# Three moves in an interleaved attention pipeline: a merge and its sum one step later in odd slots, and two SBUF elementwise operations from VectorE to GpSimd

## The chip, the cores and the metric

The kernel runs on 1 core of one Trainium2 chip. The metric is the device time of one execution in microseconds (us). Before the change the median of 3 runs is 2411.21 us (2408.04 to 2418.13).

## The reference, cut to what matters

The input x has 16 sequences of 512 tokens of 128 numbers, in fp32. Two blocks are added to it, each of a layernorm of what came before.

```python
x = x + _L0_attn_ref(_layernorm(x), wq, wk, wv, wo)   # causal, 16 heads of 8, rotary q and k
x = x + _L0_ffn_ref(_layernorm(x), wqkv, ...)          # 2 layers, each:
    h = shift_token(x);  q, k, v = split(h @ wqkv)     # 8 heads of 64
    q = l2norm(q) * qs;  k = l2norm(k) * ksc;  q, k = rotary_xpos(q, k)
    o = local_attention(q, k, v)                       # window 64 and the one before
    x = x + o @ wo
    h = layernorm(shift_token(x)) * lg + lb
    a, g = split(h @ w1 + b1);  x = x + (a * gelu(g)) @ w2 + b2
```

The outer `x +` of the second line is what the code calls adding X1 to the output: X1 is the result of the first line, Z the running value of the two layers.

## The kernel before, in words

The 16 sequences are worked on as 8 pairs (i = 0 to 7), and a pair has 16 slots (s = 0 to 15), one for each tile of 128 tokens: two layers, two sequences (z = 0, 1), four tiles. `bodies` writes the slots out in a row for every engine: two pairs of slots that only fill the pipeline (i = -2, -1), the eight real ones, and 4 slots that empty it. A program of an engine is therefore fixed by the order of calls in the loop `for s in slots` of its block, and engines meet only in semaphores. `past(sem, value)` is a wait that turns into a trivial one at the start.

In one slot s of pair i these run interleaved:
- the second block for tile s: scores (PE L725, L734), row maxima `nm` and subtraction `PX` (DVE L1019, L1022), exp (ACT L1223), transposes (PE L554), P times V (PE L751), division (DVE L1034, L1037), and for the tile before it, s-1, the turn of the heads (`turn_o`, copied by ACT L1233 to OT), `merge` (PE L786, o @ wo) and `add_heads` (DVE L1046, adds it to Z); for tile s+3 the projection (PE L699), copied by ACT L1214 to RAW, squares (ACT L1219) and `norms` (DVE L1029); for tile s+2 on Pool `over_norms` (a power, L1408) and the two rotary products and their sum (L1384, L1395, L1401), which give RC; `unit_heads` (DVE L1012) makes QN of RC one slot later.
- in odd slots the first part of the MLP of half a sequence (`half_turn`, `gates` L801, gelus on ACT L1260, `last_chunk` L810), in even slots its second part (`ups` L819, `down` L828, `add_mlp` L1082).
- `attention_step(s, pos)`, pos = 0 to 5: the first block's causal attention of later pairs, 16 heads by 2 sequences, cut into three chunks per head (512; 384 with 128; 256 columns), one chunk per step. PE makes scores for the maximum (L587) and, 6 heads later, scores for the exponential (L600, L602) in one PSUM bank each. DVE takes the maxima (L977, `maxed`), ACT the exponentials (L1188, `exped`). With one bank for each, L587 waits for the DVE of the step before, and L600 for the ACT of the step before.
- every second slot a unit of four heads goes through its maxima on Pool (`maxima_parts`, L1365 to L1371), the transpose on PE (`turn_maxima`, L622) and P times V (L645).
- the first block's projections two pairs ahead. Their rotary rows `rope_t` are split in three bf16 parts: `next_high` (ACT L1160) rounds, `next_rest` (DVE L953, slots 3, 5, 11 and 13) subtracts what was rounded, `next_middle` (ACT L1164) rounds the rest, and `next_low` (DVE L957) the last part. Then they go out through DRAM.
- layernorms of the first block on Pool: `next_normalise` in slots 1 and 9, `first_normalise` at the end of slot 7 and in slot 15 (L1338, L1340).

The last layer's `add_mlp` also adds X1 (kept in DRAM, brought back to XR) to the result: DVE L1087, in slots 12 and 14 and in slots 0 and 2 of the next pair. `fin` tells the SP queue that XR can be stored. All DMAs that these sentences speak of are issued by SP.

Of the kernel before, what the change touches and what calls it, by code (L numbers as in the profile page):

```python
# [135 lines left out]
def tile_in(i, m):  # L136

    return lives(i, m // ITEMS)
# [32 lines left out]
def build(nc, t, out):  # L171
    with ExitStack() as ctx:
# [374 lines left out]
        def _(pe):  # L547
# [28 lines left out]
            def body(i, slots):  # L576
# [260 lines left out]
                for s in slots:  # L837
# [15 lines left out]
                    if tile_in(i, s - 1):  # L853
                        merge(s - 1)
                    attention_step(s, 1)
                    attention_step(s, 2)
# [59 lines left out]
        def _(v):  # L916
# [34 lines left out]
            def next_rest(n, z, w):  # L951
                v.wait_ge(*past(part_hi.sem[z], part_hi.at(n, w + 1)))
                v.tensor_tensor(rope_s[:, :], rope_t[:, :], qkp[:, w, 0, :], ALU.subtract).then_inc(part_res.sem[z], 1)  # L953

# [15 lines left out]
            def body(i, slots):  # L970
# [70 lines left out]
                def add_heads(m):  # L1041
                    l, z, tt = place(m)
                    src = Z[z] if l else Z_first[z]
                    v.wait_ge(*past(x_tr.sem, x_tr.at(i, m // HT - 1)))
                    v.wait_ge(*past(wo_mm.sem, wo_mm.at(i, m + 1)))
                    v.tensor_tensor(Z[z][:, tt, :], m_ps[:, 0:D], src[:, tt, :], ALU.add).then_inc(z_acc.sem, 1)  # L1046
# [31 lines left out]
                def add_mlp(p):  # L1078
# [5 lines left out]
                    if l == L - 1:  # L1084
                        v.wait_ge(*past(x1_back[h].sem, x1_back[h].at(later(i, p // PIECES), z + 1)))
                        v.wait_ge(*past(z_out.sem, z_out.at(i, p + 1)))
                        v.tensor_tensor(XR[h][:, :, :], XR[h][:, :, :], zh, ALU.add).then_inc(fin.sem[h], 1)  # L1087

                for s in slots:
# [16 lines left out]
                    if tile_in(i, s - 1):  # L1106
                        add_heads(s - 1)
                    attention_step(s, 1)
                    attention_step(s, 2)
                    if s % 8 == 3 and lives(i, 2):  # L1110
                        next_rest(two, z, 0)
                    if s % 8 == 5 and lives(i, 2):
                        next_rest(two, z, 1)
# [210 lines left out]
        def _(g):  # L1324
# [24 lines left out]

            def first_normalise(k, z):  # L1350
# [6 lines left out]
            def body(i, slots):  # L1357
# [51 lines left out]

                def tile_normalise(m):  # L1410
# [11 lines left out]
                for s in slots:  # L1422
# [3 lines left out]
                    if s % 2 == 0 and unit_in(i, s // 2 + 10):  # L1426
                        maxima_parts(s // 2 + 10)
                    if s % 8 == 1 and lives(i, 2):
                        next_normalise(later(i, 2), s // 8)
# [86 lines left out]
```

## Time and profile before

| | before |
|---|---|
| median of 3 runs | 2411.21 us |
| lowest, highest | 2408.04, 2418.13 us |
| the profiled execution's own time | 2418.14 us |
| its span | 2416.4 us |
| TensorE clock granted in it | 0.977 of full speed |
| busy: PE, DVE, ACT, Pool | 2140.1, 1698.7, 1561.1, 1826.3 us |
| instructions | 55022 |

The span is that of the instructions of one execution, the time also holds what lies around it. No engine is busy all the time, so that the table alone names no limit; it has to be looked for in the waits and in the order of one slot.

### The profile page before, as it was taken

The numbers are of one execution on the slowest core, as the hardware profiler recorded it, in microseconds if no ns is written. First come the engines' busy times: TensorE is split into PE (matmuls) and PEld (weight loads), VectorE is DVE, ScalarE is ACT, GpSimd is POOL, SyncE is SP. The second block draws the span as 40 slices with busy tenths as digits, with TensorE's granted clock in tenths as the row PEclk, the third lists the DMA queues.
The fourth block names the chain that finished last, engine by engine and source line by source line (L and its number), as shares of the span: only waits on it lengthen the run. The fifth ranks groups of instructions, "written<-read, shape, count | busy, mean of one in ns | idle before, by whom it ended". The sixth has DMA issues, their size and how long they took to land.

```text
span 2416.4 us, 55022 instructions
## 1 busy us (share of the span) xinstructions
PE 2140.1 (89%) x20736; PEld 1463.9 (61%) x20736; DVE 1698.7 (70%) x4504; ACT 1561.1 (65%) x2510; POOL 1826.3 (76%) x1743
## 2 busy tenths in 40 slices
PE   4887889999999989999999989999899999988886
PEld 1444666666666666666666656666666666665664
DVE  4766777777777877777777777777777776655553
ACT  1545666676677667667676766766676677765553
POOL 2126879797887978788797978879687887798992
PEclk9998999999999999999999999999999999999997
DMA  4222111121212211121111212121111211111010
GB/s 139 67 63 57 43 51 50 45 60 45 58 37 61 52 45 51 47 61 44 51 50 48 57 44 58 35 63 52 40 51 47 61 46 38 25 33 28 21 32 23
DMA packets 115082, 119.56 MB, mean 49 GB/s; under 512 B 31946, under 2 KB 88055, under 8 KB 114819
## 3 DMA queue, kind: packets, MB, share of 16 engines
q1 hardware_dynamic: 114818, 116.04, 18.4%
q8 instruction: 167, 2.74, 0.5%
q14 instruction: 97, 0.79, 0.1%
HBM read 55.96 MB, written 20.97 MB: 32 GB/s over the span
## 4 chain that ended last, share of the span: by engine, by line
PE 50%; DVE 20%; POOL 14%; issue 10%; ACT 4%; DMA 1%; SPq 0%; DVEq 0%; POOLq 0%; ACTq 0%
DVE ps L977 6%; PE ps L554 6%; PE ps L645 5%; PE ps L734 4%; PE ps L751 4%; PE ps L587 4%; PE ps L712 4%; PE ps L828 3%; DVE nm L1019 3%; POOL inv L1408 3%; PE ps L699 3%; PE ps L600 3%; PE ps L567 2%; PE ps L819 2%; PE ps L810 2%
## 5 line engine op out<-in xcount | busy, mean ns | idle before, releaser
L977 DVE CUSTOM_DVE_ANT_0 ps<-ps,causal 128x512 f32<-128x512 f32 (+3 forms) x1024 | 491.2, 504 | 310.0 <-PE ps L587 307.1
L1188 ACT ACTIVATE PT<-ps 128x512 f32<-128x512 f32 (+1 forms) x768 | 406.8, 534 | 362.4 <-PE ps L602 350.1
L1408 POOL TENSOR_TENSOR inv<-ss,nhalf 128x16 f32<-128x16 f32 x128 | 378.7, 2959 | 324.6 <-DVE QN L1012 320.0
L587 PE MATMUL ps<-KA,QA 72*128 72x512 bf16 (+3 forms) x1024 | 274.7, 310 | 113.7 <-DVE nmax L977 111.8
L1395 POOL TENSOR_TENSOR RS<-RAW,rot 128x512 f32<-128x512 f32 x256 | 330.1, 1311 | 0.0
L1401 POOL TENSOR_TENSOR RC<-RC,RS 128x1024 f32<-128x1024 f32 x128 | 301.4, 2355 | 18.4
L1384 POOL TENSOR_TENSOR RC<-RAW,rot 128x1024 f32<-128x1024 f32 x128 | 302.7, 2365 | 0.0
L600 PE MATMUL ps<-QA,KA 75*128 75x512 bf16 (+3 forms) x1024 | 285.5, 304 | 10.6 <-ACT PT L1188 9.0
L699 PE MATMUL ps<-wqkv,ZT 128*128 128x512 f32 x512 | 241.1, 593 | 0.0
L1019 DVE TENSOR_REDUCE nm<-ps 128x8 f32<-128x1024 f32 x128 | 156.3, 1221 | 112.3 <-PE ps L734 112.2
L587 PEld LDWEIGHTS ps<-KA,QA 72*128 72x128 bf16 x1024 | 99.3, 100 | 208.8 <-DVE nmax L977 145.5
L1029 DVE TENSOR_REDUCE ss<-SQ 128x16 f32<-128x1024 f32 x128 | 155.5, 1215 | 89.1 <-POOL inv L1408 80.9
L1247 ACT COPY V_odd<-ps 128x512 f32<-128x512 f32 x128 | 74.9, 585 | 213.0 <-PE ps L712 210.2
L602 PE MATMUL ps<-causal_t,identb 128*128 128x128 bf16 x1024 | 200.7, 222 | 0.0
L786 PEld LDWEIGHTS ps<-wo,OT 128*128 128x128 f32 x1024 | 134.1, 191 | 63.0 <-issue 57.4
L1223 ACT ACTIVATE PX<-PX 128x1024 f32<-128x1024 f32 x128 | 136.5, 1067 | 55.2 <-DVE PX L1022 54.5
L645 PE MATMUL ps<-PT,V 128*32 128x512 f32 (+3 forms) x2048 | 161.3, 458 | 8.5 <-ACT PT L1188 2.3
L1022 DVE TENSOR_TENSOR PX<-ps,nm 128x1024 f32<-128x1024 f32 x128 | 156.7, 1224 | 4.4
L1012 DVE TENSOR_TENSOR QN<-RC,inv 128x1024 f32<-128x1024 f32 x128 | 157.5, 1231 | 0.2 <-POOL RC L1401 0.2
L600 PEld LDWEIGHTS ps<-QA,KA 75*128 75x128 bf16 x1024 | 101.2, 99 | 81.2 <-ACT PT L1188 27.4
L554 PE MATMUL ps<-ident,PX 128*128 128x128 f32 x1024 | 138.5, 280 | 12.1 <-ACT PX L1223 12.1
L751 PE MATMUL ps<-V_even,PT 128*64 128x65 f32 x2048 | 147.3, 225 | 0.4
(122 smaller groups left out, 5237.3 us busy)
## 6 DMA issues: line engine op xcount, KB each, us to landing
V_even<-V_odd SPq DMA_DIRECT2D x256, 130.0 KB, 2.4
QA<-parts SPq DMA_DIRECT2D x192, 96.0 KB
KA<-parts SPq DMA_DIRECT2D x192, 96.0 KB
parts<-qkp SPq DMA_DIRECT2D x32, 384.0 KB, 3.5
X_next<-in_x SPq DMA_DIRECT2D x16, 256.0 KB, 3.1
X<-in_x SPq DMA_DIRECT2D x16, 256.0 KB, 2.9
x_kept<-X SPq DMA_DIRECT2D x16, 256.0 KB, 3.6
XR<-x_kept SPq DMA_DIRECT2D x32, 128.0 KB, 2.7
```

What stands on the lines that cost most here:

```text
L554: last = pe.transpose(dst[:, tt * P:(tt + 1) * P], src(tt), ident[:, :])
L587: last = pe.matmul(dst[:, c0:c0 + w], QA[e][0:QK_ROWS, h % UNIT, qt * P:(qt + 1) * P], KA[e][0:QK_ROWS, h % UNIT, 0:w], start=True, stop=True)
L600: pe.matmul(dst[:, c0:c0 + w], KA[e][0:ROWS, h % UNIT, kt * P:(kt + 1) * P], QA[e][0:ROWS, h % UNIT, kt * P:S], start=True, stop=False)
L645: last = pe.matmul(a_ps[32 * n:32 * (n + 1), kt * P:S], V1[z][:, kt, h * VW:h * VW + 32], PT1[:, n, c0:c0 + w], start=(kt == 0), stop=(kt ...
L699: mm = pe.matmul(ps[:, w, :], ZT[z][:, tt * P:(tt + 1) * P], wqkv[:, l, w * INNER:(w + 1) * INNER], start=True, stop=True)
L751: mm = pe.matmul(out_ps[b * WIN:(b + 1) * WIN, h // PAIR2, h % PAIR2, :], PT[:, h % 2, h // 2, b * WIN:(b + 1) * WIN], values[:, h, :], st ...
L977: ins = v.tensor_tensor_reduce(for_max(i, x)[:, c0:c0 + w], for_max(i, x)[:, c0:c0 + w], causal[:, S - w:S], -1.0, -NEG, ALU.add, ALU.min, ...
L1188: a.activation(PT1[:, h % UNIT, c0:c0 + w], for_exp(i, x)[:, 0:w], ACT.Exp, scale=SCALE1).then_inc(exped.sem, 1)
L1384: g.tensor_tensor(RC.rearrange(heads, w=2, h=H2), RAW[m % 2].rearrange(heads, w=2, h=H2), rot[:, l, tt, 0, :, :].unsqueeze(2).to_broadcast ...
L1395: ins = g.tensor_tensor(turned[:, w, :, :, :], by_half[:, w, :, :, :], table[:, w, :, :].unsqueeze(1).to_broadcast([P, H2, 2, E2 // 2]), A ...
L1401: g.tensor_tensor(RC, RC, RS, ALU.add).then_inc(added.sem, 1)
L1408: g.tensor_tensor(inv[:, :], ss[:, :], nhalf[:, :], ALU.pow).then_inc(inv_ready.sem, 1)
```

## The change

In odd slots `merge(s - 1)` on PE and `add_heads(s - 1)` on DVE come after step 1 of the causal attention instead of ahead of it; even slots keep their order. `next_rest` goes from DVE to Pool, to the start of the same slots (3, 5, 11, 13). The addition of X1 goes from DVE to Pool as `add_first`, from the even slot 2p + 4 to the start of the odd slot 2p + 5 (slots 13, 15, and 1 and 3 of the next pair). Since Z is now read by Pool, `add_heads` of the first layer waits for `fin` of the pair before.

```diff
@@ PE, the loop over slots
                     if tile_in(i, s + 3):
                         project_qk(s + 3)
-                    if tile_in(i, s - 1):
+                    if s % 2 == 0 and tile_in(i, s - 1):
                         merge(s - 1)
                     attention_step(s, 1)
+                    if s % 2 and tile_in(i, s - 1):
+                        merge(s - 1)
                     attention_step(s, 2)
@@ DVE
-            def next_rest(n, z, w):
-                v.wait_ge(*past(part_hi.sem[z], part_hi.at(n, w + 1)))
-                v.tensor_tensor(rope_s[:, :], rope_t[:, :], qkp[:, w, 0, :], ALU.subtract).then_inc(part_res.sem[z], 1)
...
                     src = Z[z] if l else Z_first[z]
+                    if l == 0:
+                        v.wait_ge(*past(fin.sem[tt // HT], fin.at(later(i, m // ITEMS - 1), z + 1)))
...
-                    if l == L - 1:
-                        v.wait_ge(*past(x1_back[h].sem, x1_back[h].at(later(i, p // PIECES), z + 1)))
-                        v.wait_ge(*past(z_out.sem, z_out.at(i, p + 1)))
-                        v.tensor_tensor(XR[h][:, :, :], XR[h][:, :, :], zh, ALU.add).then_inc(fin.sem[h], 1)
@@ DVE, the loop over slots
-                    if tile_in(i, s - 1):
+                    if s % 2 == 0 and tile_in(i, s - 1):
                         add_heads(s - 1)
                     attention_step(s, 1)
+                    if s % 2 and tile_in(i, s - 1):
+                        add_heads(s - 1)
                     attention_step(s, 2)
-                    if s % 8 == 3 and lives(i, 2):
-                        next_rest(two, z, 0)
-                    if s % 8 == 5 and lives(i, 2):
-                        next_rest(two, z, 1)
@@ Pool
+            def next_rest(n, z, w):
+                g.wait_ge(*past(part_hi.sem[z], part_hi.at(n, w + 1)))
+                g.tensor_tensor(rope_s[:, :], rope_t[:, :], qkp[:, w, 0, :], ALU.subtract).then_inc(part_res.sem[z], 1)
...
+                def add_first(p):
+                    l, z, h = half_of(p)
+                    g.wait_ge(*past(x1_back[h].sem, x1_back[h].at(later(i, p // PIECES), z + 1)))
+                    g.wait_ge(*past(z_out.sem, z_out.at(i, p + 1)))
+                    g.tensor_tensor(XR[h][:, :, :], XR[h][:, :, :], Z[z][:, h * HT:(h + 1) * HT, :],
+                                    ALU.add).then_inc(fin.sem[h], 1)
@@ Pool, the loop over slots, ahead of next_normalise and first_normalise
+                    if s % 8 in (3, 5) and lives(i, 2):
+                        next_rest(later(i, 2), s // 8, s % 8 // 4)
+                    if s % 2 and piece_in(i, (s - 5) // 2) and half_of((s - 5) // 2)[0] == L - 1:
+                        add_first((s - 5) // 2)
```

On PE, an odd slot (here slot 1 of pair 0, just after the projection L699). L587 are scores for the maximum, L600 and L602 those for the exponential, L786 the merge:

```order
 L554 MATMUL ps<-ident,ON 128x128 x4
 L699 MATMUL ps<-wqkv,ZT 128x512 x2
-L786 MATMUL ps<-wo,OT 128x128 x4
-L587 MATMUL ps<-KA,QA 128x384
-L587 MATMUL ps<-KA,QA 128x128
-L600 MATMUL ps<-QA,KA 128x384
-L602 MATMUL ps<-causal_t,identb 128x128
-L600 MATMUL ps<-QA,KA 128x128
-L602 MATMUL ps<-causal_t,identb 128x128
+L587 MATMUL ps<-KA,QA 128x384
+L587 MATMUL ps<-KA,QA 128x128
+L600 MATMUL ps<-QA,KA 128x384
+L602 MATMUL ps<-causal_t,identb 128x128
+L600 MATMUL ps<-QA,KA 128x128
+L602 MATMUL ps<-causal_t,identb 128x128
+L786 MATMUL ps<-wo,OT 128x128 x4
 L587 MATMUL ps<-KA,QA 128x256
 L600 MATMUL ps<-QA,KA 128x256
```

The merge's four matmuls went from ahead of step 1 to between step 1 and step 2 (L587 of 256 columns); nothing else moved on PE.

On DVE, slot 3 of pair 1, from QN to the maxima of step 3, first before the change:

```order
L1012 TENSOR_TENSOR QN<-RC,inv 128x1024
L1046 TENSOR_TENSOR Z<-ps,Z_first 128x128
L977 ISA ps,nmax<-ps,causal 128x384
L977 ISA nmax 128x1
L977 ISA ps,nmax<-ps,causal 128x128
L977 ISA nmax 128x1
L977 ISA ps,nmax<-ps,causal 128x256
L977 ISA nmax 128x1
L953 TENSOR_TENSOR rope_s<-rope_t,qkp 128x512
L1051 BN_STATS stats<-Z 128x6
L977 ISA ps,nmax<-ps,causal 128x512
```

and the same place of the changed kernel, whose line numbers are up to 4 lower there:

```order
L1010 TENSOR_TENSOR QN<-RC,inv 128x1024
L975 ISA ps,nmax<-ps,causal 128x384
L975 ISA nmax 128x1
L975 ISA ps,nmax<-ps,causal 128x128
L975 ISA nmax 128x1
L1046 TENSOR_TENSOR Z<-ps,Z_first 128x128
L975 ISA ps,nmax<-ps,causal 128x256
L975 ISA nmax 128x1
L1051 BN_STATS stats<-Z 128x6
L975 ISA ps,nmax<-ps,causal 128x512
```

The sum into Z went behind the maxima of step 1, and the subtraction L953 is gone from between steps 2 and 3.

On Pool, the start of the same slot 3, before the change (XN is the last work of slot 2, `ss` and `inv` open slot 3's work for tile 5):

```order
L1417 TENSOR_SCALAR XN1<-Z0,mv0,rstd0 128x64
L1417 TENSOR_SCALAR XN1<-XN1,mv0,rstd0 128x64
L1405 TENSOR_SCALAR ss<-ss 128x16
L1408 TENSOR_TENSOR inv<-ss,nhalf 128x16
L1384 TENSOR_TENSOR RC<-RAW1,rot 128x1024
```

and after it:

```order
L1422 TENSOR_SCALAR XN1<-Z0,mv0,rstd0 128x64
L1422 TENSOR_SCALAR XN1<-XN1,mv0,rstd0 128x64
L1346 TENSOR_TENSOR rope_s<-rope_t,qkp 128x512
L1412 TENSOR_TENSOR XR1<-XR1,Z1 128x256
L1403 TENSOR_SCALAR ss<-ss 128x16
L1406 TENSOR_TENSOR inv<-ss,nhalf 128x16
```

Both new operations stand there between the last work of the slot before and the opening of this one. In slots 1 and 15 only the addition stands there, in 5 and 11 only the subtraction, and in 13 both again. SP's order is the same in both kernels.

## Rows read from the trace of the kernel before

**Rows 1.** The page: busy time, share of the span and instructions per engine.
```profile
PE 2140.1 (89%) x20736; PEld 1463.9 (61%) x20736; DVE 1698.7 (70%) x4504; ACT 1561.1 (65%) x2510; POOL 1826.3 (76%) x1743
```

**Rows 2.** Waits of the whole span: who waited for whom, us in total, times, longest.
```profile
ACT PT L1188 <- PE ps L602: 350.1, 273, 5.4
POOL inv L1408 <- DVE QN L1012: 320.0, 73, 8.4
```

**Rows 3.** Timeline of PE, pair 3, slot 3: start us, us, what, idle before and releaser.
```profile
1119.16 1.05 PE L786 MATMUL ps<-wo,OT 128*128 128x128 f32 x8
...
1121.45 0.28 PE L587 MATMUL ps<-KA,QA 72*128 72x256 bf16 x1 [0.67 <-DVE nmax L977]
1121.57 0.28 PE L600 MATMUL ps<-QA,KA 75*128 75x256 bf16 x1
...
1125.68 0.39 PE L587 MATMUL ps<-KA,QA 72*128 72x384 bf16 x2 [0.86 <-DVE nmax L977]
...
1129.31 1.09 PE L810 MATMUL ps<-XT_half,w 128*85 128x256 f32 x4
```

**Rows 4.** Timeline of ACT, the same slot.
```profile
1117.26 0.60 ACT L1188 ACTIVATE PT<-ps 128x512 f32<-128x512 f32 x1 [1.88 <-PE ps L602]
...
1119.65 1.02 ACT L1214 COPY RAW<-ps 128x1024 f32<-128x1024 f32 x1
1120.81 0.60 ACT L1188 ACTIVATE PT<-ps 128x512 f32<-128x512 f32 x1
1121.94 0.39 ACT L1188 ACTIVATE PT<-ps 128x256 f32<-128x256 f32 x1 [0.53 <-PE ps L602]
...
1125.00 0.63 ACT L1164 CAST qkp<-rope_s 128x512 bf16<-128x512 f32 x1
...
1128.41 0.84 ACT L1260 ACTIVATE G<-ps,b 128x256 f32<-128x256 f32 x2
```

**Rows 5.** Timeline of ACT, pair 3, slot 7, which has no L953.
```profile
1191.05 0.60 ACT L1188 ACTIVATE PT<-ps 128x512 f32<-128x512 f32 x1 [3.54 <-PE ps L602]
...
1201.70 0.84 ACT L1260 ACTIVATE G<-ps,b 128x256 f32<-128x256 f32 x2
```

**Rows 6.** DVE L953 and L1087 by line: ns min/median/max, first and last start.
```profile
L953 DVE TENSOR_TENSOR rope_s<-rope_t,qkp x32: 682/2606/2815, 24.3 to 1868.0; 128x512 f32<-128x512 f32 x32
...
L1087 DVE TENSOR_TENSOR XR<-XR,Z x32: 424/1575/2429, 446.8 to 2413.6; 128x256 f32<-128x256 f32 x32
```

**Rows 7.** Pool L1395 and L1401 by line, the same columns.
```profile
L1395 POOL TENSOR_TENSOR RS<-RAW,rot x256: 1254/1271/1731, 203.1 to 2360.5; 128x512 f32<-128x512 f32 x128
...
L1401 POOL TENSOR_TENSOR RC<-RC,RS x128: 2343/2354/2384, 205.7 to 2362.0; 128x1024 f32<-128x1024 f32 x128
```

**Rows 8.** Timeline of Pool, pair 3, slots 2 to 3, and of DVE, slot 3.
```profile
1115.14 0.25 POOL L1405 TENSOR_SCALAR ss<-ss 128x16 f32<-128x16 f32 x1
1119.01 2.93 POOL L1408 TENSOR_TENSOR inv<-ss,nhalf 128x16 f32<-128x16 f32 x1 [3.61 <-DVE QN L1012]
1121.91 2.37 POOL L1384 TENSOR_TENSOR RC<-RAW,rot 128x1024 f32<-128x1024 f32 x1
...
1117.64 1.22 DVE L1012 TENSOR_TENSOR QN<-RC,inv 128x1024 f32<-128x1024 f32 x1
...
1122.12 2.70 DVE L953 TENSOR_TENSOR rope_s<-rope_t,qkp 128x512 f32<-128x512 f32 x1
```

**Rows 9.** Timeline of PE, pair 3, slots 2 and 8, at the transposes of the maxima.
```profile
1102.30 0.40 PE L622 MATMUL ps<-identb,nparts 128*128 128x128 bf16 x4 [0.22 <-POOL nparts L1371]
1103.20 0.28 PE L587 MATMUL ps<-KA,QA 72*128 72x256 bf16 x1 [0.50 <-DVE nmax L977]
...
1211.68 0.40 PE L622 MATMUL ps<-identb,nparts 128*128 128x128 bf16 x4 [1.68 <-POOL nparts L1371]
```

**Rows 10.** Timeline of Pool, pair 3, from slot 7's QN to slot 8.
```profile
1193.37 2.93 POOL L1408 TENSOR_TENSOR inv<-ss,nhalf 128x16 f32<-128x16 f32 x1 [5.02 <-DVE QN L1012]
...
1206.81 3.74 POOL L1340 TENSOR_SCALAR Z_first<-X,first_mv,first_rstd 128x128 f32<-128x128 f32 x4
```

## The prediction

> **What bounds the kernel now.** I read the page first [rows 1]. PE is busy 2140.1 of 2416.4 us, Pool 1826.3, DVE 1698.7, ACT 1561.1. No engine is full, and the waits say why [rows 2]: ACT waits 350.1 us for PE, Pool 320.0 us for DVE's QN. The engines take turns, so I went to one slot and followed who waits last.
>
> Take slot 3 of pair 3. PE's timeline [rows 3] has two waits for DVE, 0.67 us ahead of the 256-column scores at 1121.45 and 0.86 us ahead of step 4's at 1125.68. The first is the merge's doing: DVE's sum into Z stands in its queue ahead of the maxima of step 1, so both come after the merge (1119.16), and PE waits for them before step 2. The second is L953's: it is queued ahead of the maxima of step 3.
>
> ACT's timeline [rows 4] is what ends last. From the exponential of step 0 (1117.26) to the end of the first two gelus (1128.41 + 0.84 = 1129.25) it has two holes only. One lies between the end of RAW's copy (1119.65 + 1.02 = 1120.67) and step 1's exponential (1120.81), the other is the 0.53 us ahead of step 2's exponential (1121.94). The rest is back to back, and the last chunk's matmuls on PE start at 1129.31, 0.06 after the gelus [rows 3]. They wait for them in the code.
>
> The same stretch in slot 7, which has no L953, takes from 1191.05 to 1202.54, that is 11.49 us against 11.99 [rows 4, 5]. The difference of 0.50 is what the cast L1164 (0.63 us, with the overlap of about 0.1 that neighbours on ACT have) adds. So the 2.70 us that DVE spends in L953 [rows 8], and PE's 0.86 us behind it, add nothing to ACT's chain. **In odd slots the chain is PE step 0, then ACT up to the gelus, then PE.**
>
> **The change, part by part.**
>
> *The merge.* With it behind step 1, PE issues step 1's scores at 1119.16, and its exponential no longer waits for PE. It then starts in RAW's last 0.1 us, at 1120.57 instead of 1120.81, and ends at 1121.17. PE's step 2 scores for the exponential need that bank and start 0.06 later, as L810 did behind the gelus, at 1121.23 instead of 1121.57. The maxima of step 1 are ready earlier too: PE's 0.67 us wait goes, since nothing of the merge stands ahead of them. Step 2's exponential follows L600 by 0.37 (1121.57 to 1121.94) and comes at 1121.60. All behind it is back to back, so the gain is 1121.94 - 1121.60 = 0.34 us. Bounds: 0.24 if only the first hole closes, and 0.67, PE's whole wait, if ACT were not in the way. I take 0.34.
>
> The full pattern holds in 8 odd slots each of pairs 0 to 5 and in slots 1 to 9 of pair 6, 53 in all; later there is no first-block attention left. Slot 7 is taken out. Pool runs without a gap from slot 7's QN (inv at 1193.37) through first_normalise to the maxima of slot 8 [rows 10], and PE waits 1.68 us for it at L622 [rows 9]. QN comes before the merge, so Pool is no earlier and slot 7's gain is waited away: 7 slots less, 46 stay. 46 x 0.34 = **-15.6 us**.
>
> *next_rest off DVE.* It removes 32 operations, 0.68 us alone and 2.606 us as a median [rows 6]. By the comparison above, PE's wait is hidden behind ACT: 0. If that cover were gone, it is PE's 0.86 in 24 slots (4 in each of pairs 0 to 5), 21 us.
>
> *The addition off DVE.* 32 operations, 0.424 to 2.429 us [rows 6], at the end of even slots. What follows is the next odd slot's maxima and PX. There ACT starts its run with an exponential that waits for PE (1.88 and 3.54 us) [rows 4, 5], not for DVE, and takes PX only after two copies: 0. Without that cover it would be the excess over 0.42, at most 2.0 us in 18 slots, 36 us.
>
> *Their price on Pool.* No Pool row has these shapes. The nearest is L1395, 512 columns of two SBUF operands, 1.27 us, and L1401, 1024 columns, 2.35 [rows 7]. The line through both gives 1.27 for next_rest and 0.73 for the addition; the bounds are 0.68 (DVE's) and 2.6 (twice, for the bf16 operand) for the first. 32 x 2.0 = 64 us more on Pool, which stays below PE. In slot 3 Pool idles 3.61 us from 1115.39 until QN lets inv start at 1119.01 [rows 8]. The two operations would be done by 1115.39 + 2.0 = 1117.4, just before QN starts at 1117.64. This matters: L953 was issued at 1122.12, Pool's L1384 ran until 1121.91 + 2.37 = 1124.28, and L953 ended at 1124.82, 0.54 after that, though it takes 0.68 alone. DVE had waited for Pool's operation, and QN, which also reads two SBUF operands, would do the same. By the row the sum has nothing for this, as QN comes 0.2 later.
>
> The Trainium skill, SBUF — State Buffer, section "SBUF: two separate sides", has the pair of ports that the two engines share as an exclusive lock, held for a whole instruction against a DVE operation with two SBUF inputs. L953 agrees. By that rule too the sum stays, unless the operations are longer than 2.0 us; this is rival D.
>
> From slot 15 to slot 2 Pool has no such gap, and the addition in slot 1 makes that run 0.73 longer. In slot 2, PE waits 0.22 for Pool and then 0.50 for the maxima anyway [rows 9], and Pool is later against PE by 0.73 for the addition and 0.34 for the merge, less about 0.2 that the whole run starts earlier, so 0.85; 0.50 of it is hidden and 0.35 is left. I take a fifth of it, 0.07 a pair, because Pool meets QN once a slot in this run and waits there whether it comes early or late; the bounds are 0 and 0.35. In 6 pairs: **+0.4**.
>
> *Slot 8.* With slot 7 earlier by 0.34, QN of slot 8 falls on another part of Pool's four normalisations (3.74 us) [rows 10], and one may be held for up to half of QN's 1.22 us longer. I take +0.15 in 7 pairs, bounds -0.2 and +0.6: **+1.0**.
>
> *Ends.* At the start, where L953 takes its 682 ns [rows 6], two next_rest of the first sequence are in a bare chain, 1.27 for 0.68: +1.2. The six others there free DVE between maxima, I take -0.5, bounds 0 and 6 x 0.68. At the end the last addition is 0.73 for 0.42, +0.4 with a semaphore more. **+1.1.**
>
> *New waits.* next_middle on ACT (1125.00) [rows 4] now waits for Pool, whose next_rest is done before 1119.01. `add_heads` of the first layer waits for `fin`, which is set half a slot or more before. SP's put_out in slots 1, 3, 13 and 15 waits for Pool, with the token shifts behind it, but these wait for the sum into Z, after the merge (1119.16), and the additions are done by 1117.4.
>
> **Sum**: -15.6 + 0.4 + 1.0 + 1.1 = -13.1 us. The profiled execution took 2418.14 us and would take 2405.0; the median stands 6.9 lower, so **2398.1**.
>
> **Rivals.**
>
> *A, the forecast*, 2395 to 2402, chance 0.45.
>
> *B, PE's waits were real.* If ACT's run shrinks as well once its inputs come earlier, the four slots with L953 also lose their 0.86: 21 us more, of which I keep 12 to 19, so 2379 to 2386. For it speaks that PE has the most busy time; against it the 0.50. Chance 0.12.
>
> *C, Pool takes more of it.* Pool is unbroken from slot 15 to 2 and from 7 to 10. If PE's wait there binds as in slot 8, the gains of slots 1, 9 and 15 go too, and 24 slots of 3, 5, 11 and 13 with some of the rest stay: 24 x 0.34 = 8.2, less the 2.5 above, 2402 to 2408. Against it: in slot 2 the maxima follow 0.50 later anyway. Chance 0.20.
>
> *D, slower: QN held by Pool.* QN (1117.64) waits for Pool's operation as L953 did, and has 2.2 us of room behind 1115.39. If next_rest takes 2.6 instead of 1.27, QN comes 0.4 to 1.3 late in slots 3, 5, 11 and 13, and the maxima of step 1 behind it. PE has 0.6 of room there, since L600 waits for ACT; from a delay of 0.6 on it costs, at 1.3 it is 0.7 x 24 = 17 us, and -13.1 + 17 gives 2415. Chance 0.09.
>
> *E, nothing moves*: 2408 to 2415, the shift is waited away everywhere. Chance 0.14.
>
> **How the numbers follow.** About 0.5%, 12 us, is what a measurement of this kernel can tell from no change, so 2399.2 is the border and A lies across it: faster gets 0.7 of A and all of B, with a little off for sizes, 0.43; slower by 12 us needs D's bound and more, 0.07; the same 0.50. The range, 2386 to 2413, holds A, C, the upper edge of B, most of E and half of D. The likeliest case alone is 2395 to 2402.
>
> **What would show it.** In slot 3: PE's 0.67 wait gone, ACT's two holes of 0.14 and 0.53 down to none and about 0.3, first exponential to gelus 11.65 us instead of 11.99; the 0.86 wait gone without effect. Slot 7: the same, and L622 in slot 8 waiting 2.0 us instead of 1.68. Pool's two new operations at 1.27 and 0.73 us in its idle time, QN still at 1.22. It is wrong if slots 3, 5, 11 and 13 shorten by more than 0.5, if QN lasts longer, or if L622 in slots 0, 2 and 10 waits over a microsecond.

## The result, and the profile after

The changed kernel takes 2408.09 us (median of 20 runs, 2399.82 to 2415.84), the kernel before beside it 2415.86 us (median of 20, 2408.04 to 2421.86 but for a single run of 3579.74). The ratio is 0.9969, 95% interval 0.9958 to 0.9979: 7.5 us faster. A second comparison, of 7 runs against 18 on another chip, gave 0.9954 (0.9935 to 0.9973), 11 us. The forecast was -13.1 us and 2398.1 us. The direction and the mechanism held and the size was too large. Of the 10 us between 2398.1 and 2408.09 nearly 5 are the base, the median of only 3 runs.

The page of the changed kernel, its first lines (rows 1 show the one of before):

```profile
span 2406.2 us, 55022 instructions
...
PE 2151.2 (89%) x20736; PEld 1462.6 (61%) x20736; DVE 1597.9 (66%) x4440; ACT 1554.0 (65%) x2510; POOL 1868.8 (78%) x1807
```

DVE lost 100.8 us of busy time, though the 64 operations taken from it need only 32 x (0.68 + 0.42) = 35 us alone. The rest was time in which they were held, that is, had been issued but stood still while an operation of Pool ran; the profile counts that time as busy. Pool gained 42.5 us, less than the 32 x (1.16 + 0.73) = 60 us of what it took over, because its own operations were held less: the 256 of L1395 (now L1393) fell from a mean of 1311 to 1271 ns, 10 us in all. Its two new operations, by line (ns min/median/max), beside the forecast's 1.27 and 0.73 us:

```profile
L1346 POOL TENSOR_TENSOR rope_s<-rope_t,qkp x32: 1151/1161/1168, 24.7 to 1854.3; 128x512 f32<-128x512 f32 x32
...
L1412 POOL TENSOR_TENSOR XR<-XR,Z x32: 720/727/733, 450.7 to 2403.2; 128x256 f32<-128x256 f32 x32
```

Slot 3 of pair 3 on ACT, the answer to rows 4:

```profile
1114.93 0.60 ACT L1182 ACTIVATE PT<-ps 128x512 f32<-128x512 f32 x1 [2.17 <-PE ps L602]
...
1117.32 1.02 ACT L1208 COPY RAW<-ps 128x1024 f32<-128x1024 f32 x1
1118.21 0.63 ACT L1182 ACTIVATE PT<-ps 128x512 f32<-128x512 f32 x1
1119.28 0.38 ACT L1182 ACTIVATE PT<-ps 128x256 f32<-128x256 f32 x1 [0.43 <-PE ps L602]
...
1125.76 0.84 ACT L1254 ACTIVATE G<-ps,b 128x256 f32<-128x256 f32 x2
```

and on PE, to rows 3:

```profile
1116.83 0.38 PE L587 MATMUL ps<-KA,QA 72*128 72x384 bf16 x2
...
1117.39 1.11 PE L786 MATMUL ps<-wo,OT 128*128 128x128 f32 x8
1118.34 0.27 PE L587 MATMUL ps<-KA,QA 72*128 72x256 bf16 x1
1118.90 0.28 PE L600 MATMUL ps<-QA,KA 75*128 75x256 bf16 x1 [0.29 <-ACT PT L1182]
```

From the exponential of step 0 to the end of the first two gelus ACT takes 1114.93 to 1126.60, 11.67 us, against 11.99 before; 11.65 was forecast. The first hole is gone (the exponential of step 1 starts inside RAW's copy), the second is 0.43 instead of 0.53. PE's wait of 0.67 us for the maxima is gone; the merge now runs where PE would wait for ACT in any case.

To see where a gain stays, I measured every slot from the start of DVE's reduction `nm` (L1019 of the kernel before) to that of the next slot. From slot 4 on, most slots at full clock repeat to 0.03 us from pair to pair. The larger exceptions are slots 7 to 9 in pairs 1 and 4 (up to 0.9 us), slots 11 and 15 in pair 5 of some kernels (0.2), and slots 0 to 3, where time moves between neighbours by up to 1.4 us while their sum stays within 0.4 us. Medians over pairs 1 to 5, counting only slots that have the full clock and follow one that has, in us. The first column is the median of the sum of four slots, the first two rows each take two profiles of the kernel, and -- is where no such slot was left:

```
kernel      0 to 3     4     5     6     7     8     9    10    11    12    13    14    15
before       67.88 19.35 18.82 17.70 16.49 16.60 17.37 16.69 18.78 18.55 18.82 17.63 16.78
changed      67.14 19.36 18.50 17.70 16.17 17.22 17.04 16.67 18.42 18.56 18.50 17.48 16.61
e1_merge     67.78 19.35 18.50 17.70 16.17 17.23 17.04 16.64 18.46 18.55 18.51 17.64 16.46
e2_pool      67.86 19.34 18.86 17.70 16.52 16.57 17.38 16.69 18.78 18.56 18.83 17.48 16.94
e3_slot7     67.20    --    -- 17.70 16.52 16.58 17.05 16.67 18.43 18.56 18.50 17.48 16.61
e4_norm      67.36    --    -- 17.70 16.17 15.21 17.34 16.64 18.45 18.57 18.50 17.48 16.61
e5_all       67.32 19.35 18.50 17.50 16.17 17.22 17.04 16.56 18.45 18.55 18.50 17.46 16.43
e6_low       67.69 16.86 18.50 16.90 16.31 16.07 17.04 16.56 18.45 16.38 18.68 17.16 16.31
e7_low       67.38 16.97 18.50 17.10 16.17 17.22 17.05 16.67 18.43 16.58 18.68 17.15 16.34
e8_step2     68.35 19.36 19.10 17.70 16.77 16.46 17.64 16.64 19.05 18.57 19.10 17.48 17.21
e9_best      66.76 16.86 18.50 16.90 16.18 14.99 17.34 16.44 18.46 16.39 18.68 17.16 16.13
```

A pair of the changed kernel is 2.09 us shorter at full clock (279.38 against 281.47, the sums of the rows). The forecast says 2.2: 7 x 0.34 less 0.15 and 0.07. Slot 8 is the one place from slot 4 on that went clearly the other way, by more than forecast. The changed kernel's Pool and PE there (rows 9 and 10 show them before), in pair 3:

```profile
1203.87 4.02 POOL L1334 TENSOR_SCALAR Z_first<-X,first_mv,first_rstd 128x128 f32<-128x128 f32 x4
```

```profile
1209.02 0.40 PE L622 MATMUL ps<-identb,nparts 128*128 128x128 bf16 x4 [2.29 <-POOL nparts L1369]
```

The normalisations take 4.02 us instead of 3.74, and PE waits 2.29 instead of 1.68: 0.33 because it comes earlier, 0.28 because Pool is held by QN. In pair 4 the wait is only 1.72.

The prediction named a wait of over a microsecond at L622 in slots 0, 2 or 10 as a sign of being wrong. By that letter the sign appears: in slot 0 of pairs 4 and 5 PE waits 1.11 us there (0.86 before), and in slot 10 up to 0.82 (0.28 in most pairs before). Slots 0 to 3 of these two pairs are 0.7 us shorter all the same, and slot 10 keeps its length.

### The profile page after: what moved, and what is told of

It is laid out like the page before. It is cut to its first block, busy times and chain, and to the rows that moved or that the text cites. A ratio compares the mean times of both kernels' runs of the same rounds, so it can differ in the third digit from the quotient of the medians.

```text
span 2406.2 us, 55022 instructions
## 1 busy us (share of the span) xinstructions
PE 2151.2 (89%) x20736; PEld 1462.6 (61%) x20736; DVE 1597.9 (66%) x4440; ACT 1554.0 (65%) x2510; POOL 1868.8 (78%) x1807
## 4 chain that ended last, share of the span: by engine, by line
PE 38%; POOL 23%; ACT 14%; DVE 13%; issue 9%; DMA 1%; SPq 1%; POOLq 0%; ACTq 0%; DVEq 0%
PE ps L554 5%; POOL inv L1406 5%; PE ps L645 4%; PE ps L734 4%; POOL RS L1393 3%; DVE ps L975 3%; PE ps L828 3%; POOL RC L1399 3%; POOL RC L1382 3%; PE ps L587 3%; PE ps L600 3%; DVE nm L1017 3%; PE ps L751 3%; PE ps L712 2%; PE ps L567 2%
## 5 line engine op out<-in xcount | busy, mean ns | idle before, releaser
L587 PE MATMUL ps<-KA,QA 72*128 72x512 bf16 (+3 forms) x1024 | 275.7, 311 | 55.1 <-DVE nmax L975 52.4
L1393 POOL TENSOR_TENSOR RS<-RAW,rot 128x512 f32<-128x512 f32 x256 | 319.9, 1271 | 0.0
L600 PE MATMUL ps<-QA,KA 75*128 75x512 bf16 (+3 forms) x1024 | 287.6, 307 | 29.1 <-ACT PT L1182 28.0
L699 PE MATMUL ps<-wqkv,ZT 128*128 128x512 f32 x512 | 242.9, 597 | 0.0
L587 PEld LDWEIGHTS ps<-KA,QA 72*128 72x128 bf16 x1024 | 101.3, 100 | 165.6 <-issue 82.4
L602 PE MATMUL ps<-causal_t,identb 128*128 128x128 bf16 x1024 | 201.2, 222 | 0.0
L600 PEld LDWEIGHTS ps<-QA,KA 75*128 75x128 bf16 x1024 | 101.1, 99 | 119.5 <-ACT PT L1182 66.6
L786 PEld LDWEIGHTS ps<-wo,OT 128*128 128x128 f32 x1024 | 130.7, 193 | 37.2 <-issue 31.8
```

Source lines behind the costliest of these rows:

```text
L587: last = pe.matmul(dst[:, c0:c0 + w], QA[e][0:QK_ROWS, h % UNIT, qt * P:(qt + 1) * P], KA[e][0:QK_ROWS, h % UNIT, 0:w], start=True, stop=True)
L600: pe.matmul(dst[:, c0:c0 + w], KA[e][0:ROWS, h % UNIT, kt * P:(kt + 1) * P], QA[e][0:ROWS, h % UNIT, kt * P:S], start=True, stop=False)
L699: mm = pe.matmul(ps[:, w, :], ZT[z][:, tt * P:(tt + 1) * P], wqkv[:, l, w * INNER:(w + 1) * INNER], start=True, stop=True)
L1393: ins = g.tensor_tensor(turned[:, w, :, :, :], by_half[:, w, :, :, :], table[:, w, :, :].unsqueeze(1).to_broadcast([P, H2, 2, E2 // 2]), A ...
```

## The experiments

Each comparison is with the kernel before, run beside it on the same chip. The first four kernels ran on one chip, a1_after to e6_low on a second and the last three on a third, where the kernel before had medians of 2418.20, 2416.34 and 2417.94 us. So a difference between two changed kernels from different chips carries up to 2 us of that. The clock is the mean granted clock over a kernel's runs.

| kernel | median us (runs) | clock | ratio, 95% interval |
|---|---|---|---|
| e1_merge | 2405.37 (12) | 0.979 | 0.996 (0.994 to 0.9979) |
| e2_pool | 2416.37 (12) | 0.979 | 0.9996 (0.9983 to 1.0009) |
| e3_slot7 | 2400.59 (5) | 0.979 | 0.9931 (0.9912 to 0.9949) |
| e4_norm | 2395.23 (4) | 0.977 | 0.9907 (0.9887 to 0.9927) |
| a1_after (changed kernel) | 2406.27 (7) | 0.978 | 0.9954 (0.9935 to 0.9973) |
| b1_before (kernel before) | 2417.25 (11) | 0.979 | 1.0001 (0.999 to 1.0011) |
| e5_all | 2402.22 (6) | 0.981 | 0.994 (0.9923 to 0.9957) |
| e6_low | 2350.30 (4) | 0.986 | 0.9727 (0.9711 to 0.9743) |
| e7_low | 2369.52 (4) | 0.983 | 0.9796 (0.978 to 0.9812) |
| e8_step2 | 2431.98 (6) | 0.979 | 1.0051 (1.0033 to 1.007) |
| e9_best | 2336.08 (4) | 0.987 | 0.9656 (0.964 to 0.9671) |

**The merge alone.** The kernel before with the merge's move on PE, as here, and that of add_heads on DVE in the same words, nothing else.

```diff
-                    if tile_in(i, s - 1):
+                    if s % 2 == 0 and tile_in(i, s - 1):
                         merge(s - 1)
                     attention_step(s, 1)
+                    if s % 2 and tile_in(i, s - 1):
+                        merge(s - 1)
```

> The kernel before with the merge and add_heads of odd slots behind step 1, and nothing on Pool. Theory: the merge alone makes the slots shorter. Odd slots 5, 7, 9 and 11 of pairs 0 to 5 are shorter by 0.32 to 0.36 us as in the changed kernel (18.82 to 18.50, 16.50 to 16.17, 17.37 to 17.04, 18.78 to 18.42), slot 8 longer by 0.5 to 0.65; the warm-up does not have the 0.9 us of the slower next_rest. Whole: 7 to 12 us faster than before. Rival 1, Pool's two additions ate a part of the gain: 13 us or more, and slots 0 to 2 and 15 gain 0.3 more each than in the changed kernel. Rival 2, DVE's L953 was in the way and the gain comes half from there: slots 5 and 11 gain less than 0.2, and the whole less than 6 us.

The ratio is 0.996, 10 us. Slots 5, 7, 9 and 11 and the excess of slot 8 are those of the changed kernel to 0.04 us. Rival 2 falls: next_rest still stands on DVE in slots 5 and 11, and they gain the whole 0.32. Rival 1's 13 us lie inside the interval, but not its mechanism: slot 15 gains 0.15 more than in the changed kernel and slots 0 to 3 gain less, 0 to 0.33 us by pair (0.10 between the medians) instead of 0.65 to 0.73, so that most of the merge's gain there comes through only with the other two moves. A pair's sum is 280.05.

**The Pool moves alone.** The changed kernel with merge and add_heads of all slots ahead of step 1.

> The changed kernel with the merge and add_heads of odd slots ahead of step 1 again: only the two operations on Pool. Theory: every slot from 3 to 15 as before within 0.05 us, +0.9 us in the warm-up for the slower next_rest, +0.3 at the end, slots 0 to 2 together 0 to +0.4 a pair: 0 to 4 us slower than before. Rival 1: slower by 4 us or more, in slots 0 to 2 and 15. Rival 2: faster by 3 us or more, in slots 3, 5, 11 and 13 (18.6 to 18.3 in slots 5 and 11 with the merge in its old place).

No difference: 0.9996. Slots 5, 11 and 13 are as before, so DVE's next_rest, held or not, was hidden there, as the prediction had it. Three slots missed the 0.05: slot 14 is 0.15 us shorter, slot 15 0.16 longer, and slot 3, inside the first column, 0.1 to 0.4 longer with as much less in slots 0 to 2. The addition now opens slot 15 on Pool. A pair's sum is the same (281.50 and 281.47), but with the merge moved as well the Pool moves are worth 0.67 us a pair (280.05 to 279.38), in slots 0 to 3.

**Slot 7 left as it was.** The changed kernel with this on PE, and the same for add_heads on DVE.

```diff
-                    if s % 2 == 0 and tile_in(i, s - 1):
+                    if (s % 2 == 0 or s == 7) and tile_in(i, s - 1):
                         merge(s - 1)
                     attention_step(s, 1)
-                    if s % 2 and tile_in(i, s - 1):
+                    if s % 2 and s != 7 and tile_in(i, s - 1):
                         merge(s - 1)
```

> The changed kernel with the merge and add_heads of slot 7 alone ahead of step 1 again. Theory: slot 8's excess comes from slot 7's shift (the normalisations then meet QN of slot 8 elsewhere), so slot 7 is 16.50 and slot 8 16.60 us again, 0.29 us a pair less than in the changed kernel, 2 us in 7 pairs. Rival: slot 8 stays at 17.2 because something else holds it (the addition, next_rest), and the whole is 2.3 us slower than the changed kernel.

Slot 7 is 16.52 and slot 8 16.58 again: the excess is slot 7's own shift. Moving the merge in slot 7 costs 0.29 us a pair. The whole is 6 to 8 us below the changed kernel (5 runs), more than these 2 us. Its mean clock is higher, and the rest lies within what single comparisons scatter.

**first_normalise where Pool idles.** Nothing is left out; it only stands at the start of slot 7 instead of its end.

```diff
-                    if s == 15 and lives(i, 1):
-                        first_normalise(later(i, 1), 1)
+                    if s in (7, 15) and lives(i, 1):
+                        first_normalise(later(i, 1), s // 8)
...
-                    if s == 7 and lives(i, 1):
-                        first_normalise(later(i, 1), 0)
```

> The changed kernel with first_normalise of the first sequence at the start of slot 7 on Pool, where it idles 5.02 us for QN, instead of at the end of slot 7. Theory: Pool's chain ahead of slot 8's maxima is what PE waits 2.29 us for; with it gone slot 8 falls from 17.22 to between 14.9 and 15.5 us, and inv of slot 7 starts up to 2.2 us later without effect on slot 7. 7 pairs: 12 to 16 us faster than the changed kernel, 20 to 26 faster than before. Rival: the later inv of slot 7, or DVE's QN against the normalisations, takes the place of the wait, and slots 7 and 8 together gain less than 0.8 us (under 6 us in all).

Slot 8 falls to 15.21 us, 2.0 less, and slot 7 does not move. PE at the transposes of the maxima in pair 3, slot 8:

```profile
1202.80 0.40 PE L622 MATMUL ps<-identb,nparts 128*128 128x128 bf16 x4 [0.17 <-POOL nparts L1369]
```

The wait of 2.29 us became 0.17. The medians are 11 to 13 us apart, where 12 to 16 was expected: slot 9 gives 0.3 back, and in pairs 0 and 1 slot 8 is 16.06. There the DMA that stores X1, for which first_normalise waits, lands 3.4 to 3.6 us after the start of slot 7 instead of 2.1 to 2.4, so that the normalisations start at 4.25, behind QN, which starts at 3.0 (e9_best takes this up). So Pool's unbroken run into slot 8 was the bound there, as rows 9 and 10 said.

**The two kernels once more.**

> The changed kernel once more, beside the kernel before, for the granted clock of both in every run. Theory: at one granted clock the change is worth what the slots say, 10 to 13 us, and the 7.5 us that were measured are less because the changed kernel spends more of its time at 1.2 GHz (mean 0.9765 against about 0.9786 of the kernel before, some 1.4 us for each 0.001). So its runs fall on a line of time over clock 10 to 13 us below that of the kernel before. Rival: the lines lie 7 us or less apart, so that the moves themselves are worth less than the slots of the one profile showed.

> The kernel before against itself. Theory: ratio 1.000 within 0.002, and a second profile with the same slots to 0.03 us wherever the clock was full (slot 5 18.82, slot 8 16.60, slot 11 18.78), with the stretches at 1.2 GHz in other places than in the first profile. Rival: the slots themselves differ by more than 0.1 us between two profiles of one kernel, so that differences of 0.3 us a slot say little.

The kernel before repeats itself: 1.0001, and from slot 4 on every full-clock slot to 0.04 us in the same pair. So the slot table from slot 4 on is far finer than the totals, which scatter by 15 us; slots 2 and 3 trade up to 0.2 us, and their sum repeats to 0.1. What scatters with the totals is the granted clock. Over 27 runs of the changed kernel the time falls as the clock rises, with a correlation of -0.93 and 1.6 us for each 0.001 (2415.4 us at 0.972, 2395.1 at 0.984). At equal clock the kernels compare so, means of the runs in us, for the levels with at least three runs of each:

```
clock    before        changed
0.976    2418.4 (3)    2408.0 (3)
0.977    2421.1 (10)   2407.8 (3)
0.979    2416.7 (17)   2405.8 (4)
0.980    2415.9 (12)   2403.9 (3)
```

That is 10.4 to 13.3 us, the size that the slots give. But the mean clock is 0.9790 for the kernel before (52 runs on three chips) and 0.9770 for the changed one, and 0.002 is worth some 3 us by that line. In the first comparison, the one with 7.5 us, the changed kernel had 0.9765 and no clock is recorded for the kernel before; in the second the two had 0.9783 and 0.9793, which is worth 1.6 us. The rival with 7 us falls. That the clock makes the time, and does not only go with it, is argued from these runs and from the stretches below, not tried by a run of its own.

The profile shows where it goes. PE at 1.2 GHz comes in single short stretches; the windows view of the changed kernel has slot 8 of pair 1, slot 12 of pairs 1 and 2, slot 8 of pair 3 (us, busy time and count of each engine, then PEclk):

```profile
641.00:659.46 18.46, 15.95 (x150) 11.91 (x153) 12.41 (x41) 10.55 (x18) 17.78 (x20) 0.91 0.23 61
711.89:730.75 18.86, 16.85 (x150) 11.97 (x148) 14.15 (x36) 10.61 (x18) 12.36 (x9) 0.91 0.16 40
991.72:1010.57 18.85, 16.85 (x150) 11.96 (x148) 14.22 (x36) 10.66 (x18) 12.37 (x9) 0.91 0.15 39
1202.22:1219.44 17.22, 14.71 (x154) 10.65 (x157) 12.71 (x42) 10.29 (x18) 16.61 (x17) 1.00 0.23 58
```

The same slot 12 of pair 2 in e3_slot7, whose instructions in this slot are the same:

```profile
992.02:1010.57 18.55, 15.58 (x154) 11.03 (x156) 15.36 (x35) 11.14 (x18) 12.36 (x9) 1.00 0.22 57
```

The mean clock 0.91 of a slot of 18.9 us is one stretch at half clock in it. What it costs depends on the place: slots 8 and 9 together 1.5 us (18.46 + 17.34 against 17.22 + 17.04), slots 12 and 13 0.5, slot 4 of pair 1 nothing (19.36, with and without). One that lies across slots 4 and 5, in pair 4, costs 1.6 (19.81 + 19.68 against 19.36 + 18.50). The changed kernel had one in slot 12 in pairs 1 to 5, and in its second profile in pairs 1 to 3; e3_slot7 had none there. Ahead of the one in slot 8 of pair 1, PE had waited 2.3 us for Pool; in pair 3 it waited as long and kept the full clock. Why the changed kernel draws more of them in slot 12 than e3_slot7 is not settled: the instructions of the slot are the same, what differs is when the slot comes. Nor is it settled that it always draws more than the kernel before: in pairs 0 to 6 the one before has 7 stretches in both of its profiles, the changed one 10 and 6.

**The merge in even slots too.**

```diff
-                    if s % 2 == 0 and tile_in(i, s - 1):
-                        merge(s - 1)
                     attention_step(s, 1)
-                    if s % 2 and tile_in(i, s - 1):
+                    if tile_in(i, s - 1):
                         merge(s - 1)
```

> The changed kernel with the merge and add_heads behind step 1 in even slots too. In slots 4, 6, 12 and 14 PE waits 1.10 to 1.50 us for the maxima of step 1, which stand behind add_heads (0.28 us) on DVE, and ACT has a hole of 0.9 there. Theory (who is queued ahead of step 1's maxima is what counts): these four slots become 0.28 us shorter each, the other even slots 0 to 0.3, 5 to 10 us less than the changed kernel. Rival: in even slots ACT's later work decides, and they stay as they are (within 2 us of the changed kernel).

0.994, and 279.04 against 279.38 us a pair: 2 us in 6 pairs. Slot 6 gains 0.20, slot 10 0.11, slot 15 0.18, and slots 0 to 3 lose 0.18. Slots 4, 12 and 14 gain next to nothing. The theory failed for these three, and the rows say why for slots 4 and 12; slot 14 stays open. Pool and DVE in pair 3, slot 4, which starts at 1129.09, and PE behind them:

```profile
1141.33 2.35 POOL L1395 TENSOR_TENSOR RC<-RC,RS 128x1024 f32<-128x1024 f32 x1
```

```profile
1141.56 2.67 DVE L949 TENSOR_TENSOR rope_t<-rope_t,rope_s 128x512 f32<-128x512 f32 x1
```

```profile
1146.18 0.67 PE L554 MATMUL ps<-ident,Z 128*128 128x128 f32 x2 [2.35 <-DVE Z L1080]
```

DVE's sum of two SBUF operands was issued 0.23 us after Pool's, and ended 0.55 after it, 2.67 us for work of 0.69. DVE's later work followed it, and PE waited 2.35 us. This slot also holds a stretch at 1.2 GHz and lasts 20.95 us; in pair 2, at full clock, the wait is 2.36. Pool's sum starts 12.22 to 12.27 us after the start of slots 4 and 12 in every profile, so whatever shortens DVE's way to it by less than needed is lost.

**next_low behind the maxima.** e6_low has first_normalise early, the merges of all slots behind step 1, and this:

```diff
                     if s % 8 == 4 and lives(i, 2):
                         next_cos(two, z, 1)
-                        next_low(two, z, 0)
-                    if s % 8 == 6 and lives(i, 2):
-                        next_low(two, z, 1)
                     attention_step(s, 1)
...
                         add_heads(s - 1)
+                    if s % 8 == 4 and lives(i, 2):
+                        next_low(two, z, 0)
+                    if s % 8 == 6 and lives(i, 2):
+                        next_low(two, z, 1)
```

> All at once for a faster kernel: first_normalise at the start of slot 7, the merge and add_heads behind step 1 in all slots, and next_low (0.69 us on DVE, slots 4, 6, 12 and 14) behind them instead of ahead of step 1's maxima. Theory: PE's wait of 1.10 to 1.50 us in these four slots falls by 0.28 + 0.69, of which ACT's hole of 0.9 us lets through 0.6 to 0.9; slots 4, 6, 12 and 14 are 0.6 to 0.9 us shorter, 14 to 22 us less than with first_normalise moved alone. Rival: ACT or the later maxima take it, and the four slots gain no more than 0.3 us each (7 us).

66 us less than before and 45 less than e4_norm, far beyond both theories. Slots 4 and 12 lost 2.5 and 2.2 us each. So I took next_low by itself, in the changed kernel, to right behind step 1's maxima:

> The changed kernel with next_low alone moved (DVE, slots 4, 6, 12 and 14, from ahead of step 1's maxima to behind them). In the profiles so far DVE's sum rope_t of slots 4 and 12 starts at 12.47 us or later after the start of its slot, 0.2 us or more behind Pool's sum RC (12.24), and lasts to 15.14; where next_low, the merge and add_heads were all behind the maxima it started at 11.87, took 0.78 and the slots were 2.2 to 2.5 us shorter. Theory: DVE's sum only has to be issued ahead of Pool's. next_low's 0.69 us brings it from 12.67 to 12.0 to 12.1, so it takes 0.8 us, slot 4 falls from 19.36 to 16.9 to 17.2 and slot 12 from 18.56 to 16.4 to 16.8, slots 6 and 14 by 0.2 to 0.7: 28 to 40 us less than the changed kernel. Rival: the gain came from the merges of the even slots, and slots 4 and 12 lose 0.7 us each at most (under 15 us in all).

The theory holds: 0.9796, 37 to 39 us less than the changed kernel. Slot 4 is 16.97 and slot 12 16.58. DVE's sum starts 12.07 us after the slot's start, ahead of Pool's, in pair 3, slot 4:

```profile
1121.98 0.69 DVE L951 TENSOR_TENSOR rope_t<-rope_t,rope_s 128x512 f32<-128x512 f32 x1
```

```profile
1122.16 2.72 POOL L1398 TENSOR_TENSOR RC<-RC,RS 128x1024 f32<-128x1024 f32 x1
```

Now Pool's takes 2.72 instead of 2.35: it is Pool that was held, by 0.37, and the slot is not longer for it. PE's wait for Z behind the sum, in the kernel before (pair 2, slot 4) and in e7_low (pair 3, slot 4):

```profile
868.35 0.44 PE L554 MATMUL ps<-ident,Z 128*128 128x128 f32 x2 [2.16 <-DVE Z L1082]
```

```profile
1124.63 0.44 PE L554 MATMUL ps<-ident,Z 128*128 128x128 f32 x2 [0.39 <-DVE Z L1082]
```

So 0.6 us on DVE's queue decided over 2.4 us of slot 4 and 2.0 of slot 12. DVE's sum started at 12.67 (2.48 us long) in most such slots of the first kernels and at 12.47 (2.67) in e5_all, now at 12.07 (0.69), and in e6_low at 11.87 (0.78).

The Trainium skill, SBUF — State Buffer, section "SBUF: two separate sides", says that whichever of the two operations starts first has the shared ports for its whole length and the other is blocked. Both directions are seen here, to about 0.14 us: DVE's sum of 0.69 us ended 0.55 us after Pool's and not 0.69.

**The merge one step later still.** In odd slots merge and add_heads stand behind step 2.

```diff
                     attention_step(s, 1)
+                    attention_step(s, 2)
                     if s % 2 and tile_in(i, s - 1):
                         merge(s - 1)
-                    attention_step(s, 2)
```

> The changed kernel with the merge and add_heads of odd slots behind step 2 instead of step 1. Theory: what the merge cost in its old place was the two holes in ACT's run, of 0.14 and 0.53 us, and the second is now PE's own way from the exponential of step 1 to the scores of step 2, so that nothing more is gained: odd slots 5, 7, 9 and 11 within 0.06 us of the changed kernel, the whole within 3 us. Rival: each step that the merge moves behind gains again, 0.2 us or more in each odd slot, 10 us in all.

Both were wrong: 1.0051, 24 to 26 us slower than the changed kernel. Every odd slot of the table from 5 on is 0.60 us longer than there. PE and ACT in pair 3, slot 5:

```profile
1168.61 0.28 PE L600 MATMUL ps<-QA,KA 75*128 75x256 bf16 x1 [0.44 <-ACT PT L1182]
...
1168.79 1.11 PE L786 MATMUL ps<-wo,OT 128*128 128x128 f32 x8
1169.74 1.04 PE L554 MATMUL ps<-ident,PX 128*128 128x128 f32 x8
```

```profile
1170.81 1.01 ACT L1222 COPY PT<-ps 128x1024 f32<-128x1024 f32 x1 [0.49 <-PE ps L554]
```

Behind step 2 the merge's 1.11 us stand ahead of the transposes of PX, and ACT's run gets a hole of 0.49 us. Behind step 1 most of them fill the time until step 1's exponential, which PE awaits anyhow (0.29 us of that wait are left). I had left out what is next in PE's queue.

**The fastest version.** e6_low with the wait of first_normalise for the store of X1 given to SP, ahead of the next load into that buffer.

```diff
-                g.wait_ge(*past(x1_out[z].sem, x1_out[z].now(k)))
...
                         sp.wait_ge(*past(ln_out.sem[0], ln_out.at(later(i, 1), 1)))
+                        sp.wait_ge(*past(x1_out[0].sem, x1_out[0].now(later(i, 1))))
                         load_first(1, 1)
```

The same wait, for `x1_out[1]`, stands ahead of `load_first(1, 0)`.

> The fastest kernel so far (first_normalise at the start of slot 7, merges and next_low behind step 1) with the wait for the store of X1 taken from Pool's first_normalise and put on SP ahead of the next load into X1. There Pool stands 2.1 us for that DMA, so that its first normalisation starts at 4.25 us of slot 7, behind QN. Theory: it starts at 1.5 us, Pool's work ends 1 to 1.6 us earlier, and slot 8 falls from 16.07 to about 15.2: 4 to 7 us less than the 2350.3 us of that kernel. Rival: the normalisations now meet QN (3.0 to 4.2 us) and are held through it, slot 8 gains under 0.3 us, and the whole is the same.

2336.08 us, 0.9656 (0.964 to 0.9671), 14 us less than e6_low. Slot 8 is 14.99 us, and slots 0 to 3 gain 0.9, which I had not counted: the second sequence's first_normalise, in slot 15, had waited for its store too, until 2.6 to 3.3 us after that slot's start. The forecast of 4 to 7 us was at most half of what came. Pool in pair 3, slot 7, which starts at 1142.73 (the normalisations start 1.45 us later, 1.5 forecast):

```profile
1144.18 4.21 POOL L1333 TENSOR_SCALAR Z_first<-X,first_mv,first_rstd 128x128 f32<-128x128 f32 x4
```

The rival's meeting with QN is there (4.21 us instead of 3.74), but it costs only half a microsecond of Pool's time, off the path.

## Why the prediction was right, and where its size was not

**The chain.** ACT's run from the exponential of step 0 to the gelus sets the end of an odd slot: 11.67 us, forecast 11.65. The merge's 0.34 measured 0.32 to 0.36 in slots 5, 7, 9, 11 and 13, and e1_merge has it without the Pool moves. In slot 15 it is 0.32 in e1_merge and 0.17 with the addition in that slot on Pool. The merge on PE and its sum on DVE moved together in every run, so what each gives alone was not tried; that the gain is PE's part is read from ACT's holes, which end with PE's scores.

**next_rest and the addition, 0.** Right for the two alone: e2_pool, 0.9996. Beside the merge they let 0.6 us a pair through in slots 0 to 3 (by the medians), which the forecast had already counted for the merge; it did not foresee that the merge alone would not bring it, and there the sum came out right by luck. Their price on Pool was 1.16 and 0.73 us, and QN stayed at 1.22 (median), so rival D had no ground. Rival B (12 to 19 us more) falls by slots 5 and 11 of e1_merge, rival E by the slot table.

**Slot 8.** Forecast +0.15 with slot 7's gain waited away. Measured: slots 7 and 8 together +0.30 in the medians of a pair, though nothing in pair 4. The term "+1.0" should have been about +2.0; the prediction named the cause (QN over Pool's normalisations) and took half its size. This is rival C's mechanism, confined to one slot. e3_slot7 shows that the merge of slot 7 is better left alone.

**The ends, +1.1.** At the end 0.32 us more from the last sum of Z to the end of the addition (forecast 0.4). In the warm-up the first slot starts at 225.1 and 224.3 us in the two profiles of before, and at 227.4 and 228.7 in those of the changed kernel, but e2_pool and e3_slot7, with the same operations in the same order there, have 223.8 and 229.0. The two profiled pairs of executions differ by 10 and 15 us: 2.2 and 4.3 lost before the first slot, 11.4 and 16.2 gained from there to pair 7, 0.9 and 3.1 behind it. So the warm-up may take more than the +0.7 that the forecast has for it, but with 5 us between profiles of one order the term stays open.

**The step that failed** is the last one, from the sum to the forecast: "The profiled execution took 2418.14 us and would take 2405.0; the median stands 6.9 lower". The first half held: the two profiled executions of the changed kernel took 2408.0 and 2402.5 us. The second half took the gap of one profile to a median of 3 runs as constant. With 20 runs the median of before is 2415.86, so 4.7 us of the miss is the base. Inside the sum, the term for slot 8 was too small by half, and there is no term for the granted clock, nor a reason for leaving it out. The change itself, -13.1 forecast, is -10 to -13 at equal clock. The changed kernel was granted 0.9770 instead of 0.9790 over all runs, worth some 3 us as an estimate by the line of time over clock, and 1.6 in the comparison where both clocks are on record. From 13.1, 1.0 for slot 8 and 1.6 to 3 for the clock leave 9 to 10.5; the two comparisons gave 7.5 (5 to 10) and 11 (7 to 16). Why the changed kernel is granted less, and the 1.5 us or more that are missing from the first comparison, stay open.

## What to carry to other kernels

Where VectorE and GpSimd both have operations on SBUF operands, look at their start times, not only at waits: a held operation is listed as busy and long (2.48 us for 0.69 here). A small shift of its queue can be worth nothing (0.2 us in e5_all) or most of the other's 2.35 us (0.6 us in e7_low gave 2.0 to 2.4). Price a moved block by what is queued behind its new place: the same 1.1 us of matmuls gained 0.3 us a slot behind step 1, and behind step 2 the slot was 0.6 us longer than that. Where the changes are below 0.5%, compare slots at full clock, and runs at equal granted clock, before believing a total.

## What was not expected of the hardware

The hold was in the kernel before all along, on an operation that the change does not touch. DVE and Pool in pair 2, slot 4:

```profile
863.93 2.47 DVE L949 TENSOR_TENSOR rope_t<-rope_t,rope_s 128x512 f32<-128x512 f32 x1
```

```profile
863.50 2.35 POOL L1401 TENSOR_TENSOR RC<-RC,RS 128x1024 f32<-128x1024 f32 x1
```

The hold itself is worth at most 2.48 - 0.69 = 1.8 us in each of 12 slots (4 and 12 in pairs 0 to 5), some 21 us, more than the whole change; the rest of the 2.0 to 2.5 us that these slots lost is next_low's own move. The median of that line, 0.69 us, hides it. The hold also explains why a stretch at 1.2 GHz in slot 4 of pair 1 cost nothing: the slot's end hangs on the end of Pool's operation, and DVE's came later (14.34 us after the start instead of 12.67) and shorter (0.80 us), and ended at the same 15.14. In e5_all, where DVE's sum starts 0.2 us earlier, a stretch in slot 4 did cost, 1.6 us (20.95 against 19.35). With the hold and Pool's run into slot 8 gone, the granted clock rose from 0.979 to 0.987 (e9_best). PE waits less there, but that this is the cause was not tried by itself.
